# Attention: the next context turned by four VectorE stream transposes and a pass through memory that moves the blocks, in place of 16 TensorE transposes

## The chip, the cores and the metric

One core of one Trainium2 chip runs the whole program. The metric is the device time of one execution in microseconds (us). Engines are named as in the profile: PE is TensorE, PEld its weight loads, DVE is VectorE, ACT is ScalarE, POOL is GpSimd, SP is SyncE, which here only issues transfers.

## The reference

Sixteen batches of 512 rows and 512 columns go through one layer: cross-attention with 16 heads (queries from the layer-normed `x`, keys and values from `ctx_1024`), then a feed-forward block with ternary weights. Cut to the attention half, which is all that changes:

```
qh = heads(layernorm(x) @ Wq.T);  kh = heads(ctx @ Wk.T);  vh = heads(ctx @ Wv.T + bv)
scores = (qh @ kh.T) / sqrt(32), -inf on and above the diagonal except at [0, 0]
x = x + merge(softmax(scores) @ vh) @ Wo.T + bo
x = x + ffn(layernorm(x))        # second phase of the kernel, untouched
```

Both operands of a matmul need their contraction axis on the partitions, so the context of every batch has to be turned: `cT[d, t] = ctx[t, d]`, four tiles of 128 by 512.

## The kernel before

`attention_phase` runs 16 batches, then `ffn_phase` runs 16 batches. Numbers are fp32, and each matmul operand is split in a high part (an ACT copy to fp32r, which rounds) and a low part (a DVE subtraction), so a product is three matmuls.

The work of a batch is a list of steps written out by hand, `batch_steps`. Every engine walks the same list and does its own share of each step; between engines only semaphores order the work. The list is a loop body: 15 times with work for the next batch in it (`STEADY`), and once without (`LAST`). The steps that matter here, in list order:

- `V 0..3`, `Q g`, `K g` (with their `PART` thirds): products from `cT` or `xT`, 12 matmuls each. `K 0` and `Q 0` are those of the *next* batch.
- `S g u` (scores, row maxima by DVE), `M g` (maxima turned on PE, split by ACT and DVE), `SEND g` (their transfer to the stack), `T g u` (transposed scores on PE, then `exp` on ACT, then a triangular select on POOL), ten units `u` for each of the four head groups `g`.
- `ONES g`: row sums from `acc`, which POOL builds by adding `probs` after `T g 4` and `T g 9`, for `g` = 0, 1, 2.
- `PV g r`, `NC`, `NT`, `NR`, `NB`, `NM`, `NH`, `NL`: the weighted values of a group, its normalisation, and the split into `attn`; `attn` of groups 0 and 1 reuses tiles 0 and 1 of `cT_hi` and `cT_lo`.
- `OA j g`, `OC j`, `OB j`: the output projection in parts; `OB` ends with DVE adding `x_res` and SP storing the rows (`x2_out`).
- `X_LOAD`, `LN_*`, `XT k`: the next batch's `x` goes to `xc_rows`, is normalised there and turned by PE.
- `C_LOAD`: behind `XT 3`, the next context goes to `xc_rows` (one 1 MB transfer from SP).
- `CT k`: four PE transposes by identity (line 602) into a PSUM bank of the `mm` ring, then an ACT copy to `cT_hi[k]` and a DVE subtraction to `cT_lo[k]`. `CT 2, CT 3` stand between `T 3 9` and `OA 3 0`; `CT 0, CT 1` between `OA 2 1` and `PV 3 3`, since their tiles hold `attn` until `OA 2 1`.
- `XRES`: at the very start of a batch SP loads `x` to `x_res`, and POOL adds the bias to it (line 477, four instructions). `OB` needs it at the end of the batch.

The end of a steady list is `OA 2 1, CT 0, CT 1, PV 3 3, PV 3 2, NT 3, NR 3, NB 3, NM 3 0, NH 3 0, NM 3 1, OC 0, NL 3 0, K 0, ...`, and then `OC 1..3` and `OB 0..3` with the rest of the normalisation, which depends on `NT 3`. `K 0` waits on PE until the low part of `CT 1` is written; its own result is staged by ACT and DVE, copied to the stacks by SP, and read by `S 0 0` of the next batch.

One wait used below, in PE's program for `OA`:

```
                        if s[1] >= 2 and s[2] == 0:
                            pe.wait_ge(exp_done, i * TB + TB)
```

`OA 3 0` and `OA 2 0` write the banks that the last two `T 3` units used, and so they wait until `exp` has read those.

Of the kernel before, what the change touches and what calls it, by code (L numbers as in the profile page):

```python
# [12 lines left out]
P = 128  # L13
# [42 lines left out]
def batch_steps(more):  # L56

    steps = [
# [3 lines left out]
        ("STACK", 1, 0), ("M", 0), ("V", 2), ("SEND", 0), ("PART", "Q", 2, 0), ("STACK", 1, 1), ("PART", "Q", 2, 1),  # L62
# [26 lines left out]
    ]  # L89
    return steps if more else [s for s in steps if not is_next(s, True) and s[0] not in ("X_LOAD", "C_LOAD")]  # L90

# [22 lines left out]
def is_next(step, in_batch):  # L114

    return in_batch and (step[0] in ("LN_STATS", "LN_VAR", "LN_RSTD", "LN_NEWTON", "LN_APPLY", "XT", "CT")
                         or step[:2] in (("Q", 0), ("K", 0), ("STACK", 0)) or step[:3] == ("PART", "Q", 0))
# [76 lines left out]
def attention_phase(nc, dram, batches):  # L194
    x, ctx_in, Wq, Wk, Wv, bv, Wo, bo, x2_out = dram
    S, D = x.shape[1], x.shape[2]
# [12 lines left out]
    with ExitStack() as c:  # L209
# [3 lines left out]
        def sem(name):  # L213
            return c.enter_context(nc.semaphore(name))
# [133 lines left out]
        def _(sp):  # L348
            def stack_qk(g, b, pair):

                for h in (2 * pair, 2 * pair + 1):
                    for r, pick in enumerate(STACKED):
                        sp.dma_start(stack[g % 2][32 * r:32 * r + 32, :, h, :].bitcast(F32),
                                     stage[32 * h:32 * h + 32, pick, :].bitcast(F32)
                                     ).then_inc(qk_stacked[g % 2][pair], 16)

            def program(steps, i, first, parity):
                if i is None:
# [8 lines left out]
                for s, n, _ in jobs(steps, first, parity):  # L367
# [4 lines left out]
                    elif s[0] == "XRES":  # L372
                        wait_alone(sp, sp_passed, (mm_free, first), (x2_stored, START + i * 16 * TT))
                        sp.dma_start(x_res[:, :, :], x[bass.ds(i, 1)].rearrange("a (j p) d -> p (a j) d", p=P)
                                     ).then_inc(res_loaded, 16)
                    elif s[0] == "X_LOAD":
                        wait_alone(sp, sp_passed, (mm_full, first))
                        sp.dma_start(xc_rows[:, :, :], x[bass.ds(i + 1, 1)].rearrange("a (j p) d -> p (a j) d", p=P)
                                     ).then_inc(x_loaded, 16)
                    elif s == ("XT", 3):  # L380
                        last_xt = n
                    elif s[0] == "C_LOAD":
                        wait_alone(sp, sp_passed, (mm_full, last_xt + 1))
                        sp.dma_start(xc_rows[:, :, :], ctx_in[bass.ds(i + 1, 1)].rearrange("a (j p) d -> p (a j) d", p=P)
                                     ).then_inc(c_loaded, 16)
                    elif s[0] in ("Q", "K"):
                        staged_job[s[1]] = n
                    elif s[0] == "STACK":
                        g, pair = s[1:]
                        if pair == 0:  # L390
                            wait_alone(sp, sp_passed, (mm_free, staged_job[g] + 1))
                        if g >= 2:
                            wait_alone(sp, sp_passed, (t_full, i * TB + UNITS * (g - 2) + 5 * pair + 5))

                        stack_qk(g, b, pair)
                    elif s[0] == "OB":
                        wait_alone(sp, sp_passed, (o_free, START + i * TT + s[1] + 1))
                        sp.dma_start(x2_out[bass.ds(i * TT + s[1], 1)].rearrange("a p d -> p (a d)"),
                                     x_res[:, s[1], :]).then_inc(x2_stored, 16)
# [8 lines left out]
        def _(pool):  # L408
# [61 lines left out]
            def program(steps, i, first, parity):  # L470
                chain = None if i is None else Tally(acc_step, i * (GROUPS - 1) * 14)
                for s, n, _ in jobs(steps, first, parity):
                    if s[0] == "XRES":
                        pool.wait_ge(res_loaded, i * 16 + 16)
# [4 lines left out]
                    elif s[0] == "T":  # L479
# [13 lines left out]
        def _(pe):  # L493
# [73 lines left out]
            def program(steps, i, first, parity):  # L567
                for s, n, out in jobs(steps, first, parity):
# [26 lines left out]
                    elif s[0] in ("XT", "CT"):  # L595
                        if s == ("XT", 0):
                            pe.wait_ge(xhat_ready, b * TT + TT)
                        elif s == ("CT", 0 if i is None else 2):
                            pe.wait_ge(c_loaded, b * 16 + 16)
                        src = first_context if s[0] == "CT" and i is None else xc_rows  # L600
                        for j in range(TT):
                            last = pe.transpose(out[:, P * j:P * j + P], src[:, j, P * s[1]:P * s[1] + P], ident[:, :])
                        last.then_inc(mm_full, 1)
                    elif s[0] in ("Q", "K"):
                        w, t_hi, t_lo = (0, xT_hi, xT_lo) if s[0] == "Q" else (1, cT_hi, cT_lo)
                        if s[1] == 0 and part in (None, 0):

                            pe.wait_ge(mm_free, transposed[s[0]] + 1 if i is not None else n)
                        g = s[1]
# [61 lines left out]
                    elif s[0] == "OA":  # L671
# [6 lines left out]
                        if s[1] >= 2 and s[2] == 0:  # L678
                            pe.wait_ge(exp_done, i * TB + TB)
                        out_part(s[1], (s[2],))  # L680
                    elif s[0] == "OC":
# [6 lines left out]
                    if s[0] in ("XT", "CT"):  # L688
                        transposed["Q" if s[0] == "XT" else "K"] = n

                if steps is SETUP:
                    pe.wait_ge(mm_free, MM0)

            transposed, begun, v_job = {}, {}, {}
            pe.sem_inc(ones_done, START)
# [3 lines left out]
        def _(act):  # L699
            def program(steps, i, first, parity):  # L700
                chain = Tally(act_self, 0 if i is None else i + 1)
                for s, n, out in jobs(steps, first, parity):
# [11 lines left out]
                    elif s[0] in ("W", "XT", "CT", "Q", "K"):  # L714
# [44 lines left out]
        def _(dve):  # L759
            def program(steps, i, first, parity):  # L760
# [3 lines left out]
                for s, n, out in jobs(low_parts_later(steps), first, parity):  # L764
# [101 lines left out]

            dve.sem_inc(o_free, START)
            dve.sem_inc(sums_read, START)
            in_loop(dve, program)

# [519 lines left out]
def xattn_ffn_kernel(nc, x, ctx_1024, Wq, Wk, Wv, bv, Wo, bo, fast_b, w_fc, w_proj, u, v, gate, out):  # L1391
    batches = x.shape[0]
    tiles = batches * x.shape[1] // P
    x2 = nc.dram_tensor("x2", [tiles, P, x.shape[2]], F32, kind="Internal").ap()
    attention_phase(nc, (x, ctx_1024, Wq, Wk, Wv, bv, Wo, bo, x2), batches)
    ffn_phase(nc, (x2, fast_b, w_fc, w_proj, u, v, gate, out.rearrange("b (j p) d -> (b j) p d", p=P)), batches)
# [25 lines left out]
```

## Time and profile before

| what | value |
|---|---|
| time, median of 3 runs | 2705.21 us (2700.21 to 2708.8) |
| the profiled execution: its time, its span | 2700.74 us, 2699.0 us |
| PE busy | 2581.1 us, 96% of the span |
| PEld, DVE, ACT, POOL busy | 1916.2, 1737.9, 1029.4, 787.4 us |
| mean granted PE clock | 0.981 |
| PE transposes of line 602 that read `xc_rows` | 496, 272 ns each in the middle |

The attention phase takes the first 1580 us or so, the feed-forward phase the rest. Instructions that appear in one timeline row as `x8` were merged; the time of such a row runs from the first start to the last end. A matmul's own duration includes its pipeline, so the distance between starts says what it costs PE.

### The profile page before, as it was taken

How to read it: one execution, taken by the hardware profiler on the slowest of the kernel's cores; microseconds unless marked ns; L12 is line 12 of the kernel's file. 1: busy time of each engine (PE TensorE's matmuls, PEld its weight loads, DVE VectorE, ACT ScalarE, POOL GpSimd, SP SyncE). 2: the span in 40 equal slices, each digit the busy share in tenths (PEclk: the TensorE clock that was granted, in tenths of full speed). 3: DMA queues.
4: the chain of work that ended last, by engine and by line, in shares of the span. 5: the costliest groups of instructions: out<-in, count | busy, mean ns of one | idle time of the engine just before them, and what ended most of it. 6: DMA issues, size and time to landing. Idle time of an engine off the chain costs nothing. (4 is left out here: it accounts for less than half of the span.)

```text
span 2699.0 us, 44806 instructions
## 1 busy us (share of the span) xinstructions
PE 2581.1 (96%) x14018; PEld 1916.2 (71%) x14018; DVE 1737.9 (64%) x3406; ACT 1029.4 (38%) x1903; POOL 787.4 (29%) x1495
## 2 busy tenths in 40 slices
PE   7999999999999999999999958999999999999998
PEld 5676667667667766766776636888888888888887
DVE  4675676667567567657756565666666666666663
ACT  2433433343343344334334344333333333333332
POOL 1643554474365447446544610000000000000000
PEclk9999999999999999999999877999999999999999
DMA  4344254344425434442533341111111111111111
GB/s 142 94 129 121 68 151 117 86 110 124 126 63 156 111 84 118 117 118 78 156 106 83 95 143 47 47 47 47 47 47 47 47 47 47 47 47 47 47 47 47
DMA packets 133699, 232.36 MB, mean 86 GB/s; under 512 B 20499, under 2 KB 22547, under 8 KB 133156
## 3 DMA queue, kind: packets, MB, share of 16 engines
q1 hardware_dynamic: 129572, 230.92, 29.8%
q10 hardware_dynamic: 4096, 1.06, 0.2%
q8 instruction: 16, 0.26, 0.0%
q14 instruction: 15, 0.12, 0.0%
HBM read 96.64 MB, written 33.55 MB: 48 GB/s over the span
## 5 line engine op out<-in xcount | busy, mean ns | idle before, releaser
L742 ACT ACTIVATE probs<-bank 128x512 f32<-128x512 f32 x640 | 359.0, 596 | 306.9 <-PE bank L534 299.9
L1143 PE MATMUL h_bank<-x2T_hi,fcT 128*128 128x512 f32 x1024 | 406.4, 397 | 0.9 <-ACT scale_row L1219 0.9
L1144 PE MATMUL h_bank<-x2T_lo,fcT 128*128 128x512 f32 x1024 | 406.9, 397 | 0.0
L1155 PE MATMUL y_bank<-projT,a_hi 128*128 128x512 f32 x1024 | 404.3, 395 | 0.0
L1157 PE MATMUL y_bank<-projT,a_lo 128*128 128x512 f32 x1024 | 403.9, 394 | 0.0
L1227 ACT ACTIVATE relu<-h_bank,scale_fc 128x512 f32<-128x512 f32 x256 | 176.1, 688 | 517.4 <-PE h_bank L1147 517.4
L435 POOL TENSOR_SCALAR_AFFINE_SELECT probs<-probs 128x256 f32<-128x256 f32 (+1 forms) x640 | 228.1, 367 | 242.9 <-ACT probs L742 236.6
L509 PE MATMUL bank<-stack 96*128 96x512 f32 (+3 forms) x1024 | 266.9, 338 | 18.5 <-DMA stack<-stage 14.7
L534 PE MATMUL bank<-stack 98*128 98x512 f32 (+3 forms) x1024 | 265.6, 343 | 15.8 <-DMA stack<-m_stage 15.1
L804 DVE TENSOR_REDUCE maxima<-bank 128x1 f32<-128x512 f32 x256 | 175.7, 686 | 138.2 <-PE bank L513 134.8
L1342 DVE CAST a_hi<-act_sq 128x512 fp32r<-128x512 f32 x256 | 108.4, 423 | 240.6 <-ACT act_sq L1232 240.6
L534 PEld LDWEIGHTS bank<-stack 98*128 98x128 f32 x1024 | 173.7, 194 | 90.5 <-ACT probs L742 46.9
L477 POOL TENSOR_TENSOR x_res<-x_res,bias_sb 128x512 f32<-128x512 f32 x64 | 80.5, 1289 | 519.8 <-DMA x_res<-in_x_dram 487.8
L509 PEld LDWEIGHTS bank<-stack 96*128 96x128 f32 x1024 | 178.9, 194 | 72.6 <-issue 28.5
L1144 PEld LDWEIGHTS h_bank<-x2T_lo,fcT 128*128 128x128 f32 x1024 | 193.3, 189 | 47.2
L1143 PEld LDWEIGHTS h_bank<-x2T_hi,fcT 128*128 128x128 f32 x1024 | 193.1, 189 | 47.3 <-issue 1.1
L1155 PEld LDWEIGHTS y_bank<-projT,a_hi 128*128 128x128 f32 x1024 | 192.3, 188 | 46.3
L1157 PEld LDWEIGHTS y_bank<-projT,a_lo 128*128 128x128 f32 x1024 | 192.1, 188 | 45.9
L727 ACT ACTIVATE stage<-bank 128x512 fp32r<-128x512 f32 x128 | 76.5, 598 | 316.6 <-PE bank L500 291.7
L453 POOL TENSOR_TENSOR acc<-probs 128x384 f32<-128x384 f32 x192 | 189.8, 1009 | 11.7 <-POOL probs L435 7.4
L1344 DVE TENSOR_TENSOR a_lo<-act_sq,a_hi 128x512 fp32r<-128x512 f32 x256 | 177.2, 692 | 8.8
L807 DVE TENSOR_REDUCE maxima<-bank 128x1 f32<-128x384 f32 x256 | 141.4, 552 | 56.2 <-PE bank L513 53.1
(189 smaller groups left out, 4872.6 us busy)
## 6 DMA issues: line engine op xcount, KB each, us to landing
stack<-stage SPq DMA_DIRECT2D x768, 128.0 KB, 2.3
xc_rows<-in_x_dram SPq DMA_DIRECT2D x16, 1024.0 KB, 5.3
x_res<-in_x_dram SPq DMA_DIRECT2D x16, 1024.0 KB, 5.4
x<-x_res SPq DMA_DIRECT2D x64, 256.0 KB, 2.2
x_in_sb<-x SPq DMA_DIRECT2D x16, 1024.0 KB, 5.7
x_res<-x SPq DMA_DIRECT2D x16, 1024.0 KB, 7.8
out_dram<-y_sb SPq DMA_DIRECT2D x64, 256.0 KB, 2.0
xc_rows<-in_ctx_dram SPq DMA_DIRECT2D x15, 1024.0 KB, 5.3
```

Source lines behind the costliest of these rows:

```text
L435: return pool.affine_select(out=view, in_=view, compare_op=ALU.is_ge, fill=0.0, base=0 if first_block else -1, pattern=([[0, count]] if co ...
L453: chain.inc(pool.tensor_tensor(acc[:, h, P:S], probs[:, u0, P:S], probs[:, u1, 0:S - P], ALU.add))
L509: pe.matmul(out[:, cols:cols + t1], st[0:96, QS, h, P * r:P * r + P], st[0:96, KS, h, 0:t1], start=start, stop=False, skip_group_check=True)
L534: return pe.matmul(out[:, cols:cols + S - P * r], st[0:98, KS, h, P * r:P * r + P], st[0:98, QS, h, P * r:S], start=True, stop=True)
L742: act.activation(probs[:, s[2], :], t_bank[u % 2][:, :], ACT.Exp, scale=SCALE).then_inc(exp_done, 1)
L804: last = dve.tensor_reduce(maxima[:, col + 3:col + 4], bank_u[:, :], AX.X, ALU.max)
L1143: pe.matmul(h_bank[b % 2][:, :], fcT[:, k, cols], xT_hi[:, k, :], start=k == 0, stop=False)
L1144: pe.matmul(h_bank[b % 2][:, :], fcT[:, k, cols], xT_lo[:, k, :], start=False, stop=False)
L1155: pe.matmul(y_bank[j][:, :], a_hi[:, b % RING, P * j:P * j + P], projT[:, b, :], start=b == 0, stop=False)
L1157: last = pe.matmul(y_bank[j][:, :], a_lo[:, b % RING, P * j:P * j + P], projT[:, b, :], start=False, stop=b == NB - 1)
L1227: act.activation(relu[:, b % 2, :], h_bank[b % 2][:, :], ACT.Relu, scale=scale_fc[:, b:b + 1]).then_inc(relu_done, 1)
L1344: dve.tensor_tensor(a_lo[:, b % RING, :], act_sq[:, b % 2, :], a_hi[:, b % RING, :].bitcast(F32), ALU.subtract).then_inc(hid_ready, 1)
```

## The change

Per steady batch:

- The 16 PE transposes (`CT`) go. `CT` stays in the setup, for batch 0.
- `C_LOAD` moves to the start of the batch (behind `V 0`) and loads into `acc`; it waits for the `ONES` of the batch before.
- `CTURN 0..3` are new: four DVE stream transposes, each of 128 by 512, from `acc` to `x_res`. They turn every block of 32 by 32 within its own group of 32 partitions, and stand behind `S 0 9`, behind `M 0` (two) and behind `V 2`. `CTURN 0` waits for the load and for the stores of the batch before from `x_res`. POOL waits for all four before it writes `acc` again (`T 0 4`).
- `C_STORE` is new, behind `X_LOAD` on SP: `x_res` goes to a scratch tensor in memory (1 MB). `C_BACK` takes the old place of `C_LOAD` and reads it back to `xc_rows` in four transfers of 256 KB, each to 32 partitions, with the blocks in their places (runs of 2 KB).
- `CH k` takes over ACT's copy and DVE's subtraction from `CT k`; both read `xc_rows` in SBUF, where `CT` read a PSUM bank. `CH 2, CH 3` keep their place; `CH 0, CH 1` stand behind `PV 3 2`, and ACT waits in `CH 0` for `OA 2 1`. `K 0` on PE waits for the four subtractions (`c_ready`).
- `XRES` moves behind `C_BACK`, since `x_res` is in use before; POOL's bias additions become the step `XBIAS`, behind `T 3 9`.

```diff
@@ batch_steps
-        ("XRES",), ("V", 0), ("S", 0, 0), ...
+        ("V", 0), ("C_LOAD",), ("S", 0, 0), ...
-        ... ("S", 0, 9), ("PART", "V", 1, 1), ("V", 1),
-        ("STACK", 1, 0), ("M", 0), ("V", 2), ("SEND", 0), ...
+        ... ("S", 0, 9), ("PART", "V", 1, 1), ("CTURN", 0), ("V", 1),
+        ("STACK", 1, 0), ("M", 0), ("CTURN", 1), ("CTURN", 2), ("V", 2), ("CTURN", 3), ("SEND", 0), ...
-        ("T", 0, 0), ("T", 0, 1), ("X_LOAD",), ("S", 1, 0), ...
+        ("T", 0, 0), ("T", 0, 1), ("X_LOAD",), ("C_STORE",), ("S", 1, 0), ...
-        ("PART", "Q", 0, 0), ("C_LOAD",), ("S", 3, 3), ...
+        ("PART", "Q", 0, 0), ("C_BACK",), ("XRES",), ("S", 3, 3), ...
-        ... ("T", 3, 8), ("T", 3, 9), ("CT", 2), ("NC", 2), ("CT", 3), ("OA", 3, 0), ...
+        ... ("T", 3, 8), ("T", 3, 9), ("XBIAS",), ("CH", 2), ("NC", 2), ("CH", 3), ("OA", 3, 0), ...
-        ("NL", 2, 0), ("OA", 2, 1), ("CT", 0), ("CT", 1), ("PV", 3, 3), ("PV", 3, 2), ("NT", 3), ...
+        ("NL", 2, 0), ("OA", 2, 1), ("PV", 3, 3), ("PV", 3, 2), ("CH", 0), ("CH", 1), ("NT", 3), ...
@@ SP
+                    elif s[0] == "C_LOAD":
+                        wait_alone(sp, sp_passed, (ones_done, START + i * (GROUPS - 1)))
+                        load_rows(acc, ctx_in, i + 1, c_loaded)
+                    elif s[0] == "C_STORE":
+                        wait_alone(sp, sp_passed, (c_turned, i * TT + TT))
+                        sp.dma_start(c_turned_dram, x_res[:, :, :]).then_inc(c_stored, 16)
+                    elif s[0] == "C_BACK":
+                        wait_alone(sp, sp_passed, (mm_full, last_xt + 1), (c_stored, i * 16 + 16))
+                        for q in range(4):
+                            sp.dma_start(xc_rows[32 * q:32 * q + 32, :, :],
+                                         c_turned_dram[:, q, :].rearrange("(g c) e -> c g e", c=32)
+                                         ).then_inc(c_moved, 16)
@@ POOL
+                        if s[1:] == (0, 4) and steps is STEADY:
+                            pool.wait_ge(c_turned, i * TT + TT)
@@ PE
+                            if s[0] == "K" and i is not None:
+                                pe.wait_ge(c_ready, START + i * KT + KT)
@@ ACT
+                    elif s[0] == "CH":
+                        if s[1] == 2:
+                            act.wait_ge(c_moved, i * BACK + BACK)
+                        elif s[1] == 0:
+                            act.wait_ge(oa_done, i + 1)
+                        act.activation(by_32(cT_hi[:, s[1], :]), moved_tile(s[1]), ACT.Copy).then_inc(c_hi, 1)
@@ DVE
+                    elif s[0] == "CTURN":
+                        if s[1] == 0:
+                            dve.wait_ge(x2_stored, START + i * 16 * TT)
+                            dve.wait_ge(c_loaded, i * 16 + 32)
+                        dve.transpose(x_res[:, :, :].rearrange("p q (j k t) -> p j k q t", j=TT, k=KT)[:, s[1]],
+                                      acc[:, s[1], :].rearrange("p (k q t) -> p k q t", k=KT, q=4)
+                                      ).then_inc(c_turned, 1)
+                    elif s[0] == "CH":
+                        dve.wait_ge(c_hi, i * KT + (s[1] + 2) % 4 + 1)
+                        dve.tensor_tensor(by_32(cT_lo[:, s[1], :]), moved_tile(s[1]),
+                                          by_32(cT_hi[:, s[1], :]).bitcast(F32), ALU.subtract).then_inc(c_ready, 1)
```

Here `moved_tile(k)` is tile `k` of `xc_rows` in pieces of 32 columns, and `by_32` the same cut of a `cT` tile.

## Rows read from the trace of the kernel before

**Rows 1.** One steady batch: stretch, sum, PE, PEld, DVE, ACT, POOL busy, clock.
```profile
1010.00:1105.00 95.00, 92.14 (x584) 64.47 (x583) 63.59 (x128) 36.97 (x73) 48.66 (x92) 1.00 0.41 112
```

**Rows 2.** Timeline (start, time, line): `T 3`, `CT 2`, `CT 3`, `OA 3 0`.
```profile
984.37 0.69 PE L534 MATMUL bank<-stack 98*128 98x384 f32 x4
984.89 1.04 PE L602 MATMUL bank<-ident,xc_rows 128*128 128x128 f32 x8
986.03 0.47 PE L563 MATMUL bank<-wT_hi,cT_hi 128*128 128x512 f32 x1
...
984.80 1.09 ACT L742 ACTIVATE probs<-bank 128x512 f32<-128x512 f32 x2 [0.34 <-PE bank L534]
```

**Rows 3.** Timeline, PE: end of OA 2, `CT 0/1`, PV 3, `K 0`.
```profile
991.97 0.39 PE L563 MATMUL bank<-wT_hi,cT_lo 128*128 128x512 f32 x1
...
993.16 0.43 PE L554 MATMUL bank<-probs,v_sb 128*32 128x128 f32 x8
...
995.40 0.40 PE L500 MATMUL bank<-cT_hi,wT_hi 128*128 128x512 f32 x1
```

**Rows 4.** Timeline of PE in the last batch, which has no `CT` steps.
```profile
1557.41 0.69 PE L534 MATMUL bank<-stack 98*128 98x384 f32 x4
1559.08 0.47 PE L563 MATMUL bank<-wT_hi,cT_hi 128*128 128x512 f32 x1 [0.98 <-ACT probs L742]
...
1565.01 0.39 PE L563 MATMUL bank<-wT_hi,cT_lo 128*128 128x512 f32 x1
1565.33 0.42 PE L554 MATMUL bank<-probs,v_sb 128*32 128x128 f32 x8
```

**Rows 5.** Timeline, DVE and POOL, same batch: `CT` low parts, last select.
```profile
986.41 0.69 DVE L778 TENSOR_TENSOR cT_lo<-bank,cT_hi 128x512 fp32r<-128x512 f32 x1 [3.62 <-ACT cT_hi L727]
...
993.46 1.29 DVE L778 TENSOR_TENSOR cT_lo<-bank,cT_hi 128x512 fp32r<-128x512 f32 x2 [2.65 <-ACT cT_hi L727]
...
985.56 0.90 POOL L435 TENSOR_SCALAR_AFFINE_SELECT probs<-probs 128x256 f32<-128x256 f32 x2 [0.64 <-ACT probs L742]
```

**Rows 6.** Timeline, DVE and POOL, where both read SBUF.
```profile
959.79 1.14 DVE L847 TENSOR_TENSOR o_norm<-o_norm,o_recip 128x512 f32<-128x512 f32 x1
...
959.66 1.86 POOL L459 TENSOR_TENSOR acc<-acc,probs 128x256 f32<-128x256 f32 x2
```

**Rows 7.** By source line: count, duration ns min/median/max, first and last start.
```profile
L459 POOL TENSOR_TENSOR acc<-acc,probs x192: 716/732/1187, 78.6 to 1549.0; 128x256 f32<-128x256 f32 x192
...
L477 POOL TENSOR_TENSOR x_res<-x_res,bias_sb x64: 1275/1290/1302, 54.1 to 1495.3; 128x512 f32<-128x512 f32 x64
...
L1362 DVE STREAM_TRANSPOSE x_turned<-x_in_sb x240: 699/703/707, 1685.3 to 2619.8; 32x512 f32<-32x512 f32 x120
```

**Rows 8.** Timeline, batch start: maxima, `V 1` and `V 2` copies, SP.
```profile
1016.03 0.68 DVE L811 TENSOR_REDUCE maxima<-bank 128x2 f32<-128x512 f32 x1
1017.73 0.69 DVE L796 COPY v_sb<-bank 128x512 f32<-128x512 f32 x1 [1.02 <-PE bank L500]
...
1020.60 0.69 DVE L796 COPY v_sb<-bank 128x512 f32<-128x512 f32 x1 [2.00 <-PE bank L500]
...
1007.79 2.38 SPq L398 DMA_DIRECT2D x<-x_res  x4
1012.27 0.41 SPq L374 DMA_DIRECT2D x_res<-in_x_dram  x1
```

**Rows 9.** DMA issues: line, queue, count, KB each, median us from issue to landing.
```profile
xc_rows<-in_ctx_dram SPq DMA_DIRECT2D x15, 1024.0 KB, 5.3
```

**Rows 10.** Other stretches, columns as in Rows 1.
```profile
769.50:772.90 3.40, 2.16 (x18) 1.32 (x10) 1.62 (x4) 1.99 (x4) 1.85 (x4) 1.00 0.86 197
772.90:776.30 3.40, 3.40 (x15) 1.40 (x14) 1.92 (x4) 1.68 (x3) 1.02 (x2) 0.50 0.80 187
1555.70:1559.10 3.40, 2.42 (x13) 1.70 (x12) 0.86 (x2) 2.98 (x7) 1.81 (x6) 1.00 0.00 0
1559.10:1562.50 3.40, 3.40 (x21) 1.98 (x25) 1.38 (x2) 0.96 (x2) 0.40 (x1) 1.00 0.02 5
```

More of the change, by code:

```diff
@@ L58, in batch_steps @@
     steps = [
[1 row of a table removed]
[1 row of a table added]
         ("Q", 1), ("S", 0, 3), ("S", 0, 4), ("PART", "K", 1, 0), ("S", 0, 5), ("PART", "K", 1, 1), ("S", 0, 6),
[1 row of a table removed]
-        ("STACK", 1, 0), ("M", 0), ("V", 2), ("SEND", 0), ("PART", "Q", 2, 0), ("STACK", 1, 1), ("PART", "Q", 2, 1),
[1 row of a table removed]
[1 row of a table added]
+        ("STACK", 1, 0), ("M", 0), ("CTURN", 1), ("CTURN", 2), ("V", 2), ("CTURN", 3), ("SEND", 0), ("PART", "Q", 2, 0), ("STACK", 1, 1), ("PART", "Q", 2, 1),
[1 row of a table added]
         ("S", 1, 3), ("T", 0, 3), ("PART", "K", 2, 0), ("S", 1, 4), ("T", 0, 4), ("T", 0, 5), ("S", 1, 5),
@@ L89, in batch_steps @@
     ]
-    return steps if more else [s for s in steps if not is_next(s, True) and s[0] not in ("X_LOAD", "C_LOAD")]
+    moves = ("X_LOAD", "C_LOAD", "C_STORE", "C_BACK")
+    return steps if more else [s for s in steps if not is_next(s, True) and s[0] not in moves]
 def low_parts_later(steps):
@@ L114, in is_next @@
 def is_next(step, in_batch):
-    return in_batch and (step[0] in ("LN_STATS", "LN_VAR", "LN_RSTD", "LN_NEWTON", "LN_APPLY", "XT", "CT")
+    return in_batch and (step[0] in ("LN_STATS", "LN_VAR", "LN_RSTD", "LN_NEWTON", "LN_APPLY", "XT", "CTURN", "CH")
                          or step[:2] in (("Q", 0), ("K", 0), ("STACK", 0)) or step[:3] == ("PART", "Q", 0))
@@ L251, in attention_phase @@
         c_loaded = sem("c_loaded")
+        c_turned, c_stored, c_moved = sem("c_turned"), sem("c_stored"), sem("c_moved")
+        c_hi, c_ready = sem("c_hi"), sem("c_ready")
+        oa_done = sem("oa_done")
         consts_ready = sem("consts_ready")
@@ L308, in attention_phase, with moved_tile, by_32 @@
         first_context = probs[:, 4:8, :]
+        BACK = 4 * 16
+        def moved_tile(k):
+            return xc_rows[:, :, :].rearrange("p g (j k t) -> p k j g t", j=TT, k=KT)[:, k]
+        def by_32(tile):
+            return tile.rearrange("p (j g t) -> p j g t", j=TT, g=4)
         def norm_part(g, c):
@@ L355, in stack_qk, with load_rows @@
                                      ).then_inc(qk_stacked[g % 2][pair], 16)
+            def load_rows(rows, source, i, loaded):
+                sp.dma_start(rows[:, :, :], source[bass.ds(i, 1)].rearrange("a (j p) d -> p (a j) d", p=P)
+                             ).then_inc(loaded, 16)
             def program(steps, i, first, parity):
@@ L372, in program @@
                     elif s[0] == "XRES":
-                        wait_alone(sp, sp_passed, (mm_free, first), (x2_stored, START + i * 16 * TT))
+                        if steps is STEADY:
+                            wait_alone(sp, sp_passed, (c_stored, i * 16 + 16))
+                        else:
+                            wait_alone(sp, sp_passed, (x2_stored, START + i * 16 * TT))
                         sp.dma_start(x_res[:, :, :], x[bass.ds(i, 1)].rearrange("a (j p) d -> p (a j) d", p=P)
                                      ).then_inc(res_loaded, 16)
+                    elif s[0] == "C_LOAD":
+                        wait_alone(sp, sp_passed, (ones_done, START + i * (GROUPS - 1)))
+                        load_rows(acc, ctx_in, i + 1, c_loaded)
                     elif s[0] == "X_LOAD":
-                        wait_alone(sp, sp_passed, (mm_full, first))
-                        sp.dma_start(xc_rows[:, :, :], x[bass.ds(i + 1, 1)].rearrange("a (j p) d -> p (a j) d", p=P)
-                                     ).then_inc(x_loaded, 16)
+                        wait_alone(sp, sp_passed, (mm_full, first), (c_ready, START + i * KT))
+                        load_rows(xc_rows, x, i + 1, x_loaded)
                     elif s == ("XT", 3):
                         last_xt = n
[L382 to L385, printed above, removed]
+                    elif s[0] == "C_STORE":
[7 more added lines that the diff above has]
+                                         ).then_inc(c_moved, 16)
                     elif s[0] in ("Q", "K"):
@@ L472, in program @@
                 for s, n, _ in jobs(steps, first, parity):
-                    if s[0] == "XRES":
+                    if s[0] == "XBIAS":
                         pool.wait_ge(res_loaded, i * 16 + 16)
@@ L597, in program @@
                             pe.wait_ge(xhat_ready, b * TT + TT)
-                        elif s == ("CT", 0 if i is None else 2):
-                            pe.wait_ge(c_loaded, b * 16 + 16)
-                        src = first_context if s[0] == "CT" and i is None else xc_rows
+                        elif s == ("CT", 0):
+                            pe.wait_ge(c_loaded, 16)
+                        src = first_context if s[0] == "CT" else xc_rows
                         for j in range(TT):
@@ L603, in program @@
                         last.then_inc(mm_full, 1)
+                        last_xt = n
                     elif s[0] in ("Q", "K"):
@@ L606, in program @@
                         if s[1] == 0 and part in (None, 0):
-                            pe.wait_ge(mm_free, transposed[s[0]] + 1 if i is not None else n)
+                            if s[0] == "K" and i is not None:
+                                pe.wait_ge(c_ready, START + i * KT + KT)
+                            else:
+                                pe.wait_ge(mm_free, n if i is None else last_xt + 1)
                         g = s[1]
@@ L679, in program @@
                             pe.wait_ge(exp_done, i * TB + TB)
-                        out_part(s[1], (s[2],))
+                        last = out_part(s[1], (s[2],))
+                        if s[1:] == (2, 1):
+                            last.then_inc(oa_done, 1)
                     elif s[0] == "OC":
@@ L687, in program @@
                         out_part(s[1], (3,)).then_inc(o_full, 1)
-                    if s[0] in ("XT", "CT"):
-                        transposed["Q" if s[0] == "XT" else "K"] = n
                 if steps is SETUP:
                     pe.wait_ge(mm_free, MM0)
-            transposed, begun, v_job = {}, {}, {}
+            begun, v_job = {}, {}
             pe.sem_inc(ones_done, START)
@@ L867, in _ @@
             dve.sem_inc(o_free, START)
+            dve.sem_inc(c_ready, START)
             dve.sem_inc(sums_read, START)
@@ L1394, in xattn_ffn_kernel @@
     x2 = nc.dram_tensor("x2", [tiles, P, x.shape[2]], F32, kind="Internal").ap()
-    attention_phase(nc, (x, ctx_1024, Wq, Wk, Wv, bv, Wo, bo, x2), batches)
+    turned = nc.dram_tensor("c_turned", [P, 4, x.shape[2]], F32, kind="Internal").ap()
+    attention_phase(nc, (x, ctx_1024, Wq, Wk, Wv, bv, Wo, bo, turned, x2), batches)
     ffn_phase(nc, (x2, fast_b, w_fc, w_proj, u, v, gate, out.rearrange("b (j p) d -> (b j) p d", p=P)), batches)
```

2 lines of the change are left out of this document (1 added, 1 removed), and 12 rows, old and new, of the table steps.

## The prediction

> **What bounds the kernel now.** I read the busy shares first, then one steady batch as a timeline, then what each engine waited for around the removed steps. In a steady batch of 95 us PE is busy 92.1 us, DVE 63.6, POOL 48.7 and ACT 37.0, at the full clock [rows 1]. So PE sets the pace, and work taken from it looks like pure gain: 16 transposes a batch. The busy time misleads twice, though. Eight transposes are shown with 1.04 us, and a stretch that is busy may still not be the one that decides when the next step starts. So the question is put to each of the two places where `CT` stands: when could the step behind it have begun without it?
>
> Behind `CT 2, CT 3` comes `OA 3 0`, at 986.03 [rows 2]. It needs the bank that the last `T 3` unit used, that is, the last `exp` on ACT. The two last ones run from 984.80 for 1.09 us, so to 985.89, and `OA 3 0` starts 0.14 us after that. From the last row of `T` units (start 984.37) to `OA 3 0` are 1.66 us. The last batch is a control made by the kernel itself, as it has no `CT`: there the same distance is 1559.08 - 1557.41 = 1.67 us, and PE shows 0.98 us of idle time that ACT's `exp` ends [rows 4]. These eight transposes lie in the shadow of `exp`.
>
> Behind `CT 0, CT 1` comes `PV 3 3`, which waits for nothing late. From the last matmul of `OA 2 1` to `PV 3 3` are 993.16 - 991.97 = 1.19 us with the transposes [rows 3] and 1565.33 - 1565.01 = 0.32 us without them [rows 4]. These eight are on PE's path.
>
> **The change part by part**, per steady batch, in the times of the batch around 985 us.
>
> *`CT 2, CT 3` gone:* 0. The bounds are 0 and 1.66 - 0.52 = 1.14 us (the whole distance but for what the `T` units, 0.69 us with their tail of about 0.17, take). I take 0, since the control shows the same distance with and without.
>
> *`CT 0, CT 1` gone:* 1.19 - 0.32 = 0.87 us earlier for `PV 3 3`, `PV 3 2`, `OC 0` and `K 0`, if nothing else holds them. `K 0` could start at 995.40 - 0.87 = 994.53.
>
> *What now holds `K 0`:* all four low parts on DVE, the last being `CH 1`. DVE's `CT` low parts read a PSUM bank and SBUF; `CH` reads SBUF twice. At the same time POOL now runs its four bias additions (1.29 us each [rows 7]), which stood at the start of the batch and come now right behind its last select, from 986.46 [rows 5]. Where both engines read two SBUF operands, the trace shows them taking turns: DVE's `o_norm` product at 959.79 lasts 1.14 us against 0.69, the first POOL addition at 959.66 (0.73 us, the middle of its line) ending at about 960.39, and POOL's second one ends at 961.52, 0.59 us behind DVE's end at 960.93 [rows 6, 7]. So DVE ends 0.54 us behind the POOL instruction it waited for, and POOL's next ends its own length less 0.14 behind DVE. For the bias that is 1.15 us. Played through, with POOL first: bias 1 to 987.75, `CH 2` low to 988.29, bias 2 to 989.44, `CH 3` low to 989.98, bias 3 to 991.13, `NB 2` (a transpose with one operand, 0.70 us [rows 7]) meanwhile, `NM 2 0` to 991.67, bias 4 to 992.82, ACT's copy (about 0.55 us, as each of the two `exp` [rows 2]) meanwhile, `NL 2 0` to 993.36. POOL is then done. ACT may copy `CH 0` when `OA 2 1` ends (991.97 + 0.39 = 992.36), and `CH 1` behind it, to 993.5. DVE's two low parts take 1.29 us as a pair [rows 5]; from 993.3 they end at 994.6. With DVE first the end comes out within 0.1 of that. `K 0` starts at 994.63 instead of 994.53: 0.10 us of the 0.87 is given back. `OC 0` stands three matmuls (0.69 us) ahead of `K 0`, at 993.84, and has its `NL 2 0`. The chain behind `NT 3` starts where it did (994.75 before, the end of the pair [rows 5]); the parts of it that follow `K 0`'s staging move with `K 0`.
>
> *The four `CTURN`:* a stream transpose over blocks of 32 takes 0.70 us, and it takes it with strided blocks too [rows 7]. DVE stands 1.02 us before `V 1`'s copy and 2.00 before `V 2`'s [rows 8]. `CTURN 0` fits in the first gap (from 1016.63 to 1017.33, the copy being at 1017.73), `CTURN 1` and `2` in the second (1.4 of 2.00 us, less the short low part of `M 0`), `CTURN 3` behind it. Cost 0, covered by PE's `V` products; without that cover 4 x 0.70 = 2.8 us.
>
> *`C_LOAD` early:* SP ends its four stores at 1010.17 [rows 8]. The load can go out at about 1010.9 and lands 5.3 us later [rows 9], at 1016.2; `CTURN 0` can use it from 1016.63. Behind `CTURN 0` in DVE's queue stand `V 1`'s copy and the low part of `M 0`, for which `SEND 0` and then `T 0 0` wait. Margin 0.4 us, and another 0.4 before the copy is late. Bounds: 0, and, if the load could go out only when `XRES` does today, which waits until the stores have landed (1012.27 [rows 8]), 1012.27 + 5.3 = 1017.6, `CTURN 0` to 1018.3, the copy 0.6 us late. I take 0.
>
> *`C_STORE`, `C_BACK`, `XRES`:* six transfers of 1 MB a batch where there were four. SP waits in `C_STORE` for DVE with nothing behind it until `STACK 2 0`. `C_BACK` and `XRES` go out where `C_LOAD` did; `CT 2` shows no wait for that [rows 2], and 5.3 us more [rows 9] are covered by the whole of group 3's scores and group 2's `PV`. Cost 0; without that cover 5.3 us. DVE's and ACT's counts for `CT` and `CH` are equal.
>
> Sum: -0.87 + 0.10 = -0.77 us a batch, times 15 batches = -11.6 us. Setup, last batch and feed-forward: 0. Against the profiled execution's 2700.74 us that is 2689.1; that run lies 4.5 us below the median 2705.21, so for the median 2693.6 us.
>
> **The rivals.**
>
> *B, the loser stands for the whole instruction.* If DVE and POOL exclude each other for their full lengths, each exchange costs 1.29 + 0.69: bias 1 to 987.75, `CH 2` low 988.44, bias 2 989.73, `CH 3` low 990.42, bias 3 991.71, `NM 2 0` 992.40, bias 4 993.69, `NL 2 0` 994.38, `CH 0` and `CH 1` low to 995.67, `K 0` at 995.72, 0.32 us later than before. Time: 2705.2 + 15 x 0.32 = 2710. For it: eight instructions now stand against each other where there were none. Against it: the turn in [rows 6] was cheaper. The Trainium skill, "SBUF — State Buffer", section "SBUF: two separate sides", states such a lock: whichever of the two starts first has the shared ports for the whole instruction, and the other fully blocks. The trace agrees that they take turns, and shows 0.54 and 0.59 us behind the other's end where the whole instructions are 0.69 and 0.73.
>
> *C, the clock falls: slower.* The granted clock fell to half (1.2 of 2.4 GHz) for 3.4 us at 772.9, behind a stretch in which PE was busy 2.16 of 3.4 us [rows 10]. `CT 2, CT 3` keep PE busy where it would wait. If their going made the clock fall in each batch, in the stretch of `OA` and `PV`, where PE works without gaps, each fall costs half of 3.4 us: 15 x (1.7 - 0.77) = +14, 2719 us. It turns the sign once it comes in 7 of the 15 batches. Against it: the last batch has just this stretch without `CT`, PE busy 2.42 of 3.4 us, and the clock stays full [rows 10].
>
> *D, the context lands late.* Priced above: up to 0.6 us a batch, 15 x (0.6 - 0.77) = -3, 2702 us. For it: the margin is 0.4 us; against it: the load doesn't wait for the stores' landing.
>
> *E, `CT 2, CT 3` pay too,* because `exp` comes earlier in the new order: at most 15 x (0.77 + 1.14) = -29, 2676 us. Nothing ahead of `T 3 9` on ACT or PE is taken away, so little speaks for it.
>
> **How the numbers follow.** The forecast has 0.62, B 0.15, C 0.08, D 0.10, E 0.05. A measurement tells about 0.3%, 8.1 us, from no change, that is 0.54 us a batch; the forecast's own spread (0.35 to 0.87 us, 5 to 13 us) leaves about a tenth of it below that. Faster: 0.55 + E = 0.59. Slower: C and the upper end of B, 0.12. Same: 0.29. The range takes in the forecast with the spread of the medians, D and B, and leaves out C and E: 2686 to 2711; the forecast's own is 2688 to 2700.
>
> **What would show it.** Right: 0.9 to 1.0 us of idle time before `OA 3 0`, ended by ACT's `exp`; 0.32 us from `OA 2 1` to `PV 3 3`; `K 0` within 0.2 us of the end of `OC 0`; DVE's `CH 2` and `CH 3` low parts and `NM 2 0` at up to 1.2 us or more, POOL's bias additions stretched likewise; each batch 0.8 us shorter. Wrong: DVE idle before `CTURN 0` on the load or the stores; PE waiting for `CH 1` before `K 0` by more than half a microsecond; a granted clock below 1.00 behind `OA 3 0`; ACT waiting for `c_moved`.

## The result and the profile after

The changed kernel takes 2711.94 us (median of 7 runs, 2710.08 to 2719.22), the kernel before, run beside it, 2703.26 us: a ratio of 1.0036 with the interval [1.0022, 1.0049]. It is slower by 8.7 us where 11.6 us less were forecast. The profiled execution took 2710.08 us, its span is 2708.4 us.

Almost all of the forecast's steps are nevertheless there. First the timeline of PE (start, time, line), one steady batch, where `CT` stood:

```profile
987.86 0.69 PE L565 MATMUL bank<-stack 98*128 98x384 f32 x4
989.52 0.47 PE L594 MATMUL bank<-wT_hi,cT_hi 128*128 128x512 f32 x1 [0.98 <-ACT probs L782]
...
995.46 0.39 PE L594 MATMUL bank<-wT_hi,cT_lo 128*128 128x512 f32 x1
995.78 0.43 PE L585 MATMUL bank<-probs,v_sb 128*32 128x128 f32 x8
...
997.22 0.50 PE L594 MATMUL bank<-wT_hi,attn_hi 128*128 128x512 f32 x1
...
998.10 0.51 PE L531 MATMUL bank<-cT_hi,wT_hi 128*128 128x512 f32 x1
```

From the last `T 3` row to `OA 3 0` are 1.66 us, as before [rows 2], and PE now shows the 0.98 us that it waits for `exp`. `PV 3 3` starts 0.32 us behind the last matmul of `OA 2 1`, where it was 1.19 [rows 3]. From `OA 3 0` to `K 0` are 998.10 - 989.52 = 8.58 us, before 995.40 - 986.03 = 9.37 [rows 2, 3].

Then the timeline of DVE and POOL in the same batch, with `CH 2`/`CH 3`, the four bias additions and `CH 0`/`CH 1`:

```profile
989.93 3.51 DVE L874 TENSOR_TENSOR cT_lo<-xc_rows,cT_hi 128x512 fp32r<-128x512 f32 x2 [3.65 <-ACT cT_hi L767]
...
994.10 1.03 DVE L898 TENSOR_TENSOR o_norm<-o_norm,o_recip 128x512 f32<-128x512 f32 x1
...
996.76 1.28 DVE L874 TENSOR_TENSOR cT_lo<-xc_rows,cT_hi 128x512 fp32r<-128x512 f32 x2
...
989.91 6.37 POOL L506 TENSOR_TENSOR x_res<-x_res,bias_sb 128x512 f32<-128x512 f32 x4
```

The two engines hold each other up just there, and `CH 1` ends at 998.04, 0.06 us before `K 0`. Yet the batch is longer. From one `V 0` to the next it takes 94.84 us before and 95.58 after (medians of the 14 batches behind the first, which is left out: it takes 98 to 107 us over all the kernels here). So something is lost elsewhere in the batch. The waits of the steady batches name it (engine, line waited for: us in total, times, longest):

```profile
PE bank L540 <- DMA stack<-stage: 29.3, 29, 1.8
...
DVE ln_stats L160 <- DMA xc_rows<-in_x_dram: 23.4, 14, 2.1
...
PE bank L594 <- ACT probs L782: 13.7, 14, 1.0
```

In the kernel before, over the same stretch, the first two are:

```profile
PE bank L509 <- DMA stack<-stage: 13.8, 15, 1.9
...
DVE ln_stats L159 <- DMA xc_rows<-in_x_dram: 5.9, 14, 0.6
```

DVE waits four times as long for `x`, and PE waits twice as often for the stack copies. The reason stands in the DMA issues (count, KB each, median us from issue to landing; first the kernel before, then the changed one) and in the changed kernel's timeline of SP, DVE and PE around `X_LOAD`:

```profile
xc_rows<-in_x_dram SPq DMA_DIRECT2D x16, 1024.0 KB, 5.3
```
```profile
xc_rows<-in_x_dram SPq DMA_DIRECT2D x16, 1024.0 KB, 6.4
...
c_turned<-x_res SPq DMA_DIRECT2D x15, 1024.0 KB, 8.3
```
```profile
549.00 0.40 SPq L373 DMA_DIRECT2D xc_rows<-in_x_dram  x1
549.59 0.42 SPq L408 DMA_DIRECT2D c_turned<-x_res  x1
...
555.75 0.69 DVE L160 BATCH_NORM_STATS2 ln_stats<-xc_rows 128x6 f32<-128x512 f32 x1 [1.99 <-DMA xc_rows<-in_x_dram]
556.36 0.54 DVE L847 TENSOR_REDUCE maxima<-bank 128x1 f32<-128x384 f32 x1
...
557.62 0.67 DVE L844 TENSOR_REDUCE maxima<-bank 128x1 f32<-128x512 f32 x1
...
558.35 0.50 PE L540 MATMUL bank<-stack 96*128 96x256 f32 x2 [0.56 <-DVE maxima L844]
...
565.05 0.50 PE L540 MATMUL bank<-stack 96*128 96x512 f32 x1 [0.64 <-DMA stack<-stage]
```

`C_STORE` goes out 0.59 us behind `X_LOAD`, and `x` lands 6.4 us after its issue instead of 5.3. `LN_STATS 0` stands in DVE's queue ahead of row maxima of `S 1` and the low part of `K 2`. The units of `S 1` behind these maxima come late, `STACK 2 0` goes out late, and `S 2 0` waits for it. Laid against the kernel before, unit by unit from `V 0` on (medians of the 14 batches), a batch loses 0.54 us at `S 1` and 0.86 at `S 2 0`, makes up 0.27 in `S 2`, changes by -0.40, +0.20 and +0.41 at `T 2 0`, `XT 3` and `S 3 0`, gains 0.87 at `PV 3 3` and gives 0.20 back at `K 0` (0.08 ahead of its first matmul and 0.12 behind it, where the second now follows after 0.34 us and not 0.23). With 0.07 in smaller steps that is the +0.74 us.

The Trainium skill, "DMA: Bandwidth & Descriptors", section "Two DMAs through the same engine are not ordered", states that within one queue of a DMA engine descriptors start in order but are pipelined. The trace agrees with the second half: being queued 0.59 us ahead did not keep `x` from landing 1.1 us later.

### The profile page after: what moved, and what is told of

Read it like the earlier page. It is cut to its first block and busy times, and to the rows that moved or that the text cites. A ratio compares the mean times of both kernels' runs of the same rounds, so it can differ in the third digit from the quotient of the medians.

```text
span 2708.4 us, 44446 instructions
## 1 busy us (share of the span) xinstructions
PE 2560.2 (95%) x13778; PEld 1888.3 (70%) x13778; DVE 1824.5 (67%) x3466; ACT 1031.8 (38%) x1903; POOL 807.2 (30%) x1495
## 5 line engine op out<-in xcount | busy, mean ns | idle before, releaser
L585 PE MATMUL bank<-probs,v_sb 128*32 128x512 f32 (+3 forms) x2048 | 168.6, 442 | 7.2 <-POOL probs L464 7.2
```

## Experiments

Theory A: the store beside `X_LOAD` is what costs. Theory B: the lock of DVE and POOL is. Theory C: two more megabytes a batch slow the stack copies wherever they go. Ratios are to the kernel before, run on the same chip, with 95% intervals. Times from different chips are compared by their ratios.

**e1, e2: the two transfers apart.** In e1 the store stands behind `STACK 2 1`, in e2 the load goes out early instead.

```
e1: -  ("T",0,1), ("X_LOAD",), ("C_STORE",), ...   ("STACK",2,1), ("S",2,0)
    +  ("T",0,1), ("X_LOAD",), ...                 ("STACK",2,1), ("C_STORE",), ("S",2,0)
e2: -  ("C_LOAD",), ("S",0,0), ...                 ("T",0,1), ("X_LOAD",), ("C_STORE",)
    +  ("C_LOAD",), ("X_LOAD",), ("S",0,0), ...    ("T",0,1), ("C_STORE",)
```

> The changed kernel with C_STORE behind STACK 2 1 (some 16 us later, with no load near it) and nothing else moved. Theory A (C_STORE goes out 0.6 us behind X_LOAD, the two share the DMA engines, x lands 1.1 us late, DVE stands in LN_STATS 0 with row maxima and K 2's low part queued behind it, and so STACK 2 0 and S 2 0 are late): x lands after 5.3 us as before the change, DVE waits about 0.4 us in LN_STATS 0 in place of 1.7, PE's waits for the stack copies fall from 30 us in total to about 13, and the time is about 2694 us, 0.3 to 0.4% under the kernel before. Theory B (DVE and POOL lock each other out at the batch's end) : 2712 us as the changed kernel. Theory C (two more megabytes a batch slow the stack copies wherever they go): 2708 to 2712 us, PE's waits for the stack copies stay near 30 us.

> The changed kernel with X_LOAD at the start of the batch, right behind C_LOAD, and nothing else moved; C_STORE then has no load beside it. Theory A: no wait in LN_STATS 0 at all; but now the two loads share the engines, so the context lands later than its 5.4 us, and CTURN 0 may stand for up to 1 us before V 1's copy: 2694 to 2703 us. Theory B: 2712 us. Theory C: 2708 to 2712 us.

e1: 2711.66 us, ratio 1.0032 [1.0020, 1.0044]. e2: 2737.58 us, 1.0124 [1.0103, 1.0144]. In e1 the mechanism is mended: `x` lands after 5.4 us, the store after 4.1, and DVE's wait falls from 1.67 to 0.61 us a batch, near the 0.42 of the kernel before:

```profile
xc_rows<-in_x_dram SPq DMA_DIRECT2D x16, 1024.0 KB, 5.4
...
c_turned<-x_res SPq DMA_DIRECT2D x15, 1024.0 KB, 4.1
```
```profile
DVE ln_stats L160 <- DMA xc_rows<-in_x_dram: 8.6, 14, 0.8
```

The time is no shorter: it is theory C's, not the 2694 of theory A. So theory A was not the whole of it. But the stack copies land after 2.4 us in the middle, 2.3 in the kernel before, so theory C's mechanism isn't there, and e8 below, with as many bytes, is faster than the kernel before. e1's batches show what is: the short ones take 94.41 us, 0.4 less than before, but nine of the 14 take 95.2 to 97.5. In eight of those the granted clock falls to half, at one place, `S 3 0` (before it falls there in one batch, of 96.48 us). Windows of e1 (stretch, length, then busy time of PE, PEld, DVE, ACT, POOL, then the clock): first the stretch ahead of `S 3 0` and the one behind it in a batch without a fall, then the same two in the batch after it, with one.

```profile
1065.95:1069.35 3.40, 2.14 (x17) 1.01 (x17) 2.08 (x3) 2.31 (x4) 2.59 (x5) 1.00 0.87 198
...
1069.35:1072.75 3.40, 3.40 (x22) 1.98 (x23) 2.68 (x6) 1.79 (x4) 1.02 (x2) 1.00 0.85 196
...
1160.37:1163.77 3.40, 2.15 (x17) 1.02 (x17) 2.09 (x3) 2.31 (x4) 2.61 (x5) 1.00 0.88 199
1163.77:1167.17 3.40, 3.40 (x14) 1.14 (x15) 2.00 (x3) 1.71 (x3) 1.00 (x2) 0.61 0.87 199
```

The mean of 0.61 mixes full speed with half, and PE gets 14 matmuls done instead of 22. PE did as little ahead of `S 3 0` in both batches, so the idle time allows the fall and doesn't decide it alone. The nine batches exceed 94.41 us by 16.5 us in all; without that e1 would be at about 2695 us, by this estimate.

e2 fits none of the theories' times. Its `x` lands 8.6 us after issue, the context 5.8, and `SEND 0`'s rows, which go out while `x` is under way, land after 4.2 to 6.1 us where it is 2.3 in the changed kernel; PE waits up to 3.6 us for them ahead of `T 0 0`. The collision has only been moved, to a transfer with less slack.

**e3, e4: the suspects one by one.** e3 is the kernel before plus a 1 MB store of a constant right behind `X_LOAD`. e4 is the changed kernel without POOL's bias additions, so the bias is left out of the output.

```
e3: +  sp.dma_start(spare_dram, wT_lo[:, 0, :, :].bitcast(F32))      # behind X_LOAD
e4: -  for j in range(TT): pool.tensor_tensor(x_res[:, j, :], x_res[:, j, :], bias_sb[:, :], ALU.add)
    +  pool.sem_inc(xres_ready, TT)
```

> The kernel before, with one thing added: SP sends 1 MB of constant weights to a scratch tensor right behind X_LOAD, as C_STORE does in the changed kernel; nobody waits for it. Theory A: x lands after 6.4 us, DVE's wait in LN_STATS 0 grows from 0.4 to 1.7 us a batch, and the time grows by 1.1 to 1.5 us a batch, 16 to 23 us, to 2719 to 2726 us. Theory B: no change, 2703 us. Theory C: part of it, 2707 to 2712 us.

> The changed kernel without POOL's four bias additions (the output projection's bias is left out of the result; the semaphore is raised all the same). Theory A: DVE's CH 2 and CH 3 low parts fall from 1.8 to 0.69 us, K 0 comes 0.2 us a batch earlier, the waits in LN_STATS 0 stay: about 2709 us. Theory B: the whole loss goes, 2693 to 2697 us. Theory C: 2709 to 2712 us.

e3: 2724.08 us, 1.0092 [1.0077, 1.0106], as theory A expected: the store alone, with none of the rest of the change, brings the waits of the changed kernel. It takes 95.94 us a batch, 1.10 more than the kernel before.

```profile
xc_rows<-in_x_dram SPq DMA_DIRECT2D x16, 1024.0 KB, 6.2
...
spare<-wT_lo SPq DMA_DIRECT2D x15, 1024.0 KB, 8.1
```
```profile
PE bank L515 <- DMA stack<-stage: 29.4, 29, 1.9
...
DVE ln_stats L159 <- DMA xc_rows<-in_x_dram: 19.8, 14, 1.8
```

e4: 2714.41 us, 1.0050 [1.0037, 1.0063]. `K 0`'s loss of 0.20 us is gone and the batch takes 95.34 us, 0.24 less than in the changed kernel, but the time is not shorter, and 5 us above what theory A expected; two of its 14 batches show a fall of the clock, against one. Theory B, by which it would have taken 2693 to 2697 us, falls.

**e5, e6, e7: why the clock falls in e1.** The loss at `S 3 0` starts with an exchange of issues. `STACK 3 0` is issued by SP, `SEND 2` by ACT, at the same moment. Timeline of the kernel before (one issue by itself, then a pair):

```profile
957.33 0.60 SPq L353 DMA_DIRECT2D stack<-stage  x1
...
957.98 1.23 SPq L353 DMA_DIRECT2D stack<-stage  x2
...
958.11 0.51 ACTq L711 DMA_DIRECT2D stack<-m_stage  x1
958.11 1.38 ACTq L711 DMA_DIRECT2D stack<-m_stage  x2
```

and of e1:

```profile
1063.30 0.63 SPq L367 DMA_DIRECT2D stack<-stage  x1
...
1063.98 1.46 SPq L367 DMA_DIRECT2D stack<-stage  x2
...
1063.99 0.52 ACTq L745 DMA_DIRECT2D stack<-m_stage  x1
1063.99 1.16 ACTq L745 DMA_DIRECT2D stack<-m_stage  x2
```

SP's second and third issue take 1.23 us before and 1.46 in e1; ACT's pair takes 1.38 before and 1.16 in e1. Before, SP's third issue goes ahead of ACT's second; in e1 SP is some 0.1 us later and the order turns. `SEND 2` is then early (`T 2 0` by 0.37 us) and `STACK 3 0` late (`S 3 0` by 0.25 us), so that PE's idle time gathers in one long stand ahead of `S 3 0`. PE in the kernel before (`T 2 0`, `S 3 0`), then in e1 (`S 3 0`):

```profile
961.43 0.50 PE L534 MATMUL bank<-stack 98*128 98x512 f32 x1 [0.31 <-DMA stack<-m_stage]
...
963.23 0.49 PE L509 MATMUL bank<-stack 96*128 96x512 f32 x1 [0.86 <-DMA stack<-stage]
```
```profile
1069.35 0.49 PE L540 MATMUL bank<-stack 96*128 96x512 f32 x1 [1.21 <-DMA stack<-stage]
```

The changed kernel has the same 1.21, and so, within 0.04 us, have e3 to e6; all of them have SP's long third issue.
e5 is the kernel before with e3's spare store behind `STACK 2 1`. e6 and e7 are e1 with one edit each:

```
e6: +  if s[1] == 2: act.activation(pause[:, :], ones[0:1, :], ACT.Copy)      # ahead of SEND's issues
e7: +  twice = 2 if s == ("XT", 3) and steps is STEADY else 1
    -  for j in range(TT):
    +  for j in list(range(TT)) * twice:                                      # XT's transposes
```

> The kernel before with one 1 MB store added, of a constant tile, at the later place (behind STACK 2 1) instead of right behind X_LOAD. Theory A (a store costs where it runs beside X_LOAD, and nothing of its own at the later place): x lands after 5.3 to 5.5 us, the batch takes 94.8 us, 2700 to 2706 us. Rival (a further store a batch disturbs at any place: it makes SP's STACK 3 0 issues late, S 3 0 late behind them, and the clock falls there): 2712 to 2725 us.

> The store behind STACK 2 1, and before SEND 2's two issues ACT copies 128 values of one partition to a spare tile, so that SP's third STACK 3 0 issue goes ahead of ACT's second issue again. Theory A (the batch's own time is 94.4 us, and the rest of the time was lost to a clock that fell where PE stood ahead of S 3 0, because the two issues had changed places): SP's third issue takes 0.60 us again, S 3 0 starts some 0.25 us sooner, the clock falls in at most 3 batches, and the time is 2692 to 2699 us. Rival (the falls have nothing to do with the order of issues; the store or the VectorE transposes bring them): 2709 to 2716 us.

> The store behind STACK 2 1, and XT 3's four TensorE transposes done twice into the same bank, in the time in which PE stands ahead of S 3 0 anyway. Theory A (the clock falls because PE did too little there): the clock falls in at most 3 batches, and the time is 2692 to 2699 us, though the kernel does more work. Rival (the falls come from something other than PE's idle time there): 2709 to 2718 us.

e5: 2715.17 us, 1.0051 [1.0032, 1.0069]: the rival. `x` lands after 5.3 us, but SP's third issue takes 0.83 us here too, `S 3 0` is 0.23 us late, the batch takes 95.08 us, and four of 14 show a fall (96.6 to 96.7 us). So a further store costs even where it isn't in flight beside `x`, by way of the order of issues.

e6: 2713.34 us, 1.0032 [1.0019, 1.0045], which tests nothing. ACT issued `SEND 2` beside its copy, not behind it (the copy at 50.08 us of the batch, the issue at 50.09), so the order stayed as in e1, and with it the falls (nine of 14).

e7: 2695.37 us, 0.9972 [0.9962, 0.9982]: as theory A expected. Four more transposes a batch make the kernel 16 us faster than e1 (by the ratios). None of the 14 batches shows a fall, they take 94.35 to 94.72 us. Window of e7 ahead of `S 3 0`:

```profile
1055.15:1058.55 3.40, 2.59 (x22) 1.47 (x21) 2.08 (x3) 1.93 (x4) 2.59 (x5) 1.00 0.87 198
```

**e8 to e12: the order of issues put right.** Ahead of `STACK 2 0` and `3 0` SP waits for two semaphores, the staged projection first and then the `T` units, which are met long before. The edit turns them round, so that the first issue follows the later event at once.

```
e8:    if g >= 2:    wait_alone(sp, sp_passed, (t_full, ...))        # was second
       if pair == 0: wait_alone(sp, sp_passed, (mm_free, ...))       # was first
e9:  e8 with e7's XT 3      e10: the kernel before with both
e11: the changed kernel as it is, with e8's edit      e12: the kernel before with e8's edit
```

> The store behind STACK 2 1, and SP's two waits ahead of STACK 2 0 and 3 0 in the other order: first the one for the T units, which is met long before, then the one for the staged projection, so that the first issue goes out right behind the later of the two. Theory A (the clock fell because S 3 0 was late, because ACT's second SEND 2 issue went ahead of SP's third): the first issue is 0.1 us sooner, SP's third issue takes 0.60 us again, S 3 0 starts at 55.0 to 55.2 us of the batch, the clock falls in at most 3 of 14 batches, the undisturbed batch takes 94.0 to 94.4 us, and the time is 2689 to 2698 us. Rival (the order of issues is not what lets the clock fall): the falls stay, 2709 to 2716 us.

> The same with XT 3's four transposes done twice. Theory A: no falls in the 14 batches, S 3 0 at 55.0 to 55.2, 94.0 to 94.4 us a batch, 2687 to 2695 us. Rival (the two repairs do the same thing, and the order of issues sets no time of its own): as with XT 3 done twice alone, 2693 to 2698 us.

> The kernel before with the same two edits and nothing of the change: SP's waits in the other order and XT 3's transposes twice. Theory A (what the change gives is its own: 0.87 us at PV 3 3 less 0.19 us at K 0 in a batch): its batch takes 0.4 to 0.7 us more than that of the changed kernel with both edits, 2696 to 2703 us, 6 to 10 us more than that one. Rival (the gain is that of the two edits alone, the change gives nothing): 2687 to 2695 us, within 3 us of it.

> The changed kernel as it is, with C_STORE right behind X_LOAD, and only SP's two waits ahead of STACK 2 0 and 3 0 in the other order. Theory A (the early store costs time of its own, whatever the order of issues: 0.54 us at S 1 and 0.9 us at S 2 0 of each batch, of which 0.26 us are made up behind them): x lands after 6.4 us, LN_STATS waits 2 us for it, the batch takes 95.0 to 95.4 us, 2701 to 2709 us. Rival (the order of issues was the whole loss, and the late x is hidden): 94.0 to 94.2 us a batch, 2685 to 2691 us.

> The kernel before with SP's two waits in the other order and nothing else. Theory A (the order of issues was right in the kernel before, so little is won: S 3 0 some 0.15 us sooner, and the single fall of the clock gone at best): 94.65 to 94.8 us a batch, 2697 to 2703 us, 10 to 16 us more than the changed kernel with the later store and this order. Rival (the order is what made that version fast, not the change): 2686 to 2692 us.

| place of the store | waits as they were | waits turned | turned, `XT 3` twice |
|---|---|---|---|
| no store (before) | 2703.26 | e12 2695.99, 0.9979 [0.9968, 0.9990] | e10 2698.12, 0.9983 [0.9974, 0.9992] |
| beside `X_LOAD` (the change) | 2711.94, 1.0036 [1.0022, 1.0049] | e11 2705.05, 1.0011 [1.0001, 1.0021] | not run |
| behind `STACK 2 1` | e1 2711.66, 1.0032 [1.0020, 1.0044] | e8 2686.64, 0.9943 [0.9931, 0.9956] | e9 2690.46, 0.9953 [0.9940, 0.9966] |

All five came out on theory A's side, e8 and e12 a little below their ranges; e12 takes 9.4 us more than e8, where 10 to 16 were expected. Timeline of the issues in e8, and its windows: the stretch ahead of `S 3 0`, and a whole batch, to be laid beside [rows 1]:

```profile
952.76 0.62 SPq L367 DMA_DIRECT2D stack<-stage  x1
...
953.43 1.23 SPq L367 DMA_DIRECT2D stack<-stage  x2
...
953.61 0.51 ACTq L745 DMA_DIRECT2D stack<-m_stage  x1
953.61 1.31 ACTq L745 DMA_DIRECT2D stack<-m_stage  x2
```
```profile
955.24:958.64 3.40, 2.31 (x26) 1.27 (x18) 2.34 (x3) 2.12 (x5) 2.89 (x5) 1.00 0.88 200
...
997.62:1091.69 94.07, 90.40 (x566) 62.58 (x564) 68.33 (x132) 36.96 (x72) 49.94 (x92) 1.00 0.51 135
```

SP's pair takes 1.23 us again, and one of e8's 14 batches shows a fall against eight in e1; but for it and the first (95.42 us, at full clock) they take 94.04 to 94.15 us. In e9 none shows one; it is not faster than e8, nor e10 than e12, so with the order right the extra transposes have nothing left to mend. Over all kernels but e2, those whose stand ahead of `S 3 0` is 1.2 us in the middle show one to nine falls in 14 batches, those with 0.85 us or less (the kernel before, e7 to e12) none or one. e11 keeps DVE's wait for `x`:

```profile
DVE ln_stats L160 <- DMA xc_rows<-in_x_dram: 23.2, 14, 2.0
```

and takes 95.0 us a batch: the early store costs by itself, whatever the order. e12 shows what the order gives the kernel before, 94.72 us a batch; 3.1 us of its 6.6 can be seen in the 14 batches of one execution each. For the rest there is a hint in the other executions of the kernel before, whose times go with their mean granted clock, from 2695.34 us at 0.985 to 2708.26 at 0.978, as they would if the number of falls differed from one execution to the next.

## Why the prediction was wrong

**Right: PE's part.** `CT 2, CT 3` were worth nothing (1.66 us before and after), `CT 0, CT 1` 0.87 us (0.32 us from `OA 2 1` to `PV 3 3`), and from `OA 3 0` to `K 0` 8.60 us were forecast and 8.58 measured. The turns of DVE and POOL were sized right: POOL's four additions 6.36 forecast and 6.37 measured. Rival B's count by whole lengths makes them 993.69 - 986.46 = 7.23 us, so its price did not come. The Trainium skill, "SBUF — State Buffer", section "SBUF: two separate sides", states that the instruction that starts first has the shared ports for its whole length and the other fully blocks; the trace agrees that they take turns, but the turns do not add up to whole lengths. For `K 0` the sum gave back 0.10 us; 0.08 came ahead of its first matmul, and 0.12 behind it, which the sum did not count. e4 shows that the whole of the conflict is worth only these 0.20 us. The chances for "faster" add up to 0.60, not 0.59, which changes nothing.

**Right: `CTURN` and `C_LOAD`.** `CTURN` takes 0.70 us, stands in DVE's idle time and waits for the context in two of the 14 batches, 0.5 us at most; `T 0 0` starts at 19.3 us of the batch as before, so rival D did not come.

**Wrong: "`C_STORE`, `C_BACK`, `XRES`: ... Cost 0".** For `C_STORE` the step looked only at what stands behind it in SP's queue, and found nothing until `STACK 2 0`. It did not ask what is in flight ahead of it. `X_LOAD` had gone out 0.59 us before, and the step's own rule, that a transfer is covered, was never put to the transfer next to it, whose slack was nil: DVE already waited up to 0.6 us for it in the kernel before. Measured: 1.1 us on the landing, a wait of 1.67 us a batch on DVE in place of 0.42, and 1.16 us on PE by the end of `S 2`. e3 shows it without the rest of the change, and e11 against e8 in its place: 95.04 - 94.10 = 0.94 us a batch in the medians, 18.4 us in the times. (The 0.2 us between 1.16 and 0.94 go with the order of issues: with the waits turned, e11's `S 2 0` is 0.2 us earlier than the changed kernel's.) `C_BACK` and `XRES` cost nothing that was found: `XRES` lands after 8.1 us where it was 5.4, and nobody waits for it.

**Missing: the order of two queues.** That one more store turns the order of SP's and ACT's issues at `STACK 3 0` was no term of the sum. In the changed kernel it is +0.41 + 0.20 - 0.40 = +0.21 us a batch behind `S 2`; in e1 it let the clock fall in eight of 14 batches and ate all that moving the store had won. The changed kernel stays the slower one without it, though: with the waits turned in both, the change as it is (e11) takes 2705.05 - 2695.99 = 9.1 us more than the kernel without it (e12), where it was 8.7. In the batches of one execution each the difference does shrink, from 0.74 to 0.32 us, so how much the order adds to the loss is not settled. Rival C had the right mechanism at the wrong place: the clock did not fall behind `OA 3 0`, where PE lost `CT 2, CT 3`, but at `S 3 0`, where PE stood already. The fall that [rows 10] shows is at that very place, 0.9 us behind the `S 3 0` of its batch.

With both put right the change gives what was forecast, nearly: e8 against e12, the same order of waits with and without it, is 2686.64 - 2695.99 = -9.4 us, or 94.10 - 94.72 = -0.62 us a batch, against -11.6 and -0.77. (e9 against e10, both with `XT 3` twice: -7.7 us.) So with the waits turned the change splits into these -9.4 us and the 18.4 us that the store costs beside `X_LOAD`, 9.1 us together. Of the signs that the prediction had listed for being wrong only one showed, DVE's wait for the context, and only in two batches; it had listed none for `X_LOAD`.

Open: why SP's first issue is 0.1 us later in all the kernels with one more store (in the changed kernel, e1, e3 and e5, though SP had been idle for long), and why the same stand of 1.21 us ahead of `S 3 0` lets the clock fall in one of 14 batches of the changed kernel and in eight of e1.

## What to carry to other kernels

A new transfer is priced against the transfers in flight beside it, and against the slack of whoever waits for those, not only against what is queued behind it. Where two engines issue DMAs at the same moment, 0.1 us can turn their order: put the wait that is met last right ahead of the first issue. When a repair shows in the waits but not in the time, look at the granted clock batch by batch before the theory is given up; work for an engine that stands anyway may pay for itself, as in e7, though no longer once the stand is short (e9, e10).

## What was not expected of the hardware

A 1 MB store issued 0.59 us behind a 1 MB load delayed the load's landing from 5.3 to 6.4 us, and took 8.3 us itself where it takes 4.1 with no load beside it. Two DMA issues of SP and ACT that meet cost the loser some 0.2 us (0.60 to 0.83). ACT issues a DMA while its own copy is under way. And a kernel with four more TensorE transposes a batch was 16 us faster than the one without, because the clock then stayed at full speed.
